# The first FFN and the input projection as bodies of one block, with waits at first use in place of the barrier between them

## What is computed

```python
x = x + 0.5 * ffn(layernorm(x))                 # weights = lut[idx], 256 -> 688 -> 256
x = x + mamba(layernorm(x))                     # the step in the middle
x = x + 0.5 * ffn(layernorm(x))                 # the same weights again

def ffn(x):    return (silu(x @ W_gate.T) * (x @ W_up.T)) @ W_down.T
def mamba(x):
    proj = x @ in_proj_w * mup                  # 256 -> z 512, xBC 768, dt 64
    xBC  = silu(causal_conv4(xBC) + conv_b)     # per channel, 4 taps
    dt   = softplus(dt + dt_bias)
    # scan over 2048 tokens, 64 heads of 8, state of 128; then + D * x,
    # rms norm, norm_w, * silu(z)
    return y @ out_proj_w                       # 512 -> 256
```

## Time and profile before

| what | value |
|---|---|
| median of 3 runs | 519.86 us (518.34 to 520.81) |
| the profiled execution | 518.19 us |
| its span, first to last instruction | 516.5 us |
| mean granted TensorE clock | 0.98 |
| PE busy | 473.5 us, 92% |
| DVE busy | 374.7 us, 73% |
| ACT busy | 284.0 us, 55% |
| GpSimd busy | 160.9 us, 31% |

### The profile page before, as it was taken

One profiled execution on the slowest core, in us unless ns is written; L12 is line 12 of the kernel. 1 busy time (PEld: TensorE's weight loads), 2 busy tenths in 40 slices (PEclk: granted clock), 3 DMA queues, 4 the chain that ended last, 5 costly groups with the idle time before them and its releaser, 6 DMA issues.

```text
span 516.5 us, 17146 instructions
## 1 busy us (share of the span) xinstructions
PE 473.5 (92%) x7486; PEld 396.9 (77%) x7486; DVE 374.7 (73%) x742; ACT 284.0 (55%) x513; POOL 160.9 (31%) x216
## 2 busy tenths in 40 slices
PE   4899999999989995986899999999978999999997
PEld 3557797988878884875688878887867778898987
DVE  7998936466769999844788888788859866556543
ACT  3658535253328999798556665567635423323241
POOL 1100040203042111114667676676746411000000
PEclk9999999999989999797999999999989999999999
DMA  8960080000000000100000000000350000101001
GB/s 206 207 241 1 1 339 7 0 3 1 0 1 0 3 0 0 42 22 3 4 6 4 5 4 6 4 5 4 134 220 4 4 2 0 42 7 35 22 21 42
DMA packets 7387, 21.31 MB, mean 41 GB/s; under 512 B 784, under 2 KB 5392, under 8 KB 6672
## 3 DMA queue, kind: packets, MB, share of 16 engines
q1 hardware_dynamic: 6832, 18.05, 10.7%
q10 hardware_dynamic: 480, 2.16, 1.8%
HBM read 12.87 MB, written 6.55 MB: 38 GB/s over the span
## 4 chain that ended last, share of the span: by engine, by line
PE 32%; issue 9%; POOL 8%; ACT 4%; DVE 3%; POOLq 0%; DVEq 0%; ACTq 0%
POOL w L1264 6%; PE intra L898 4%; PE seg L876 2%; PE yo L1016 2%; POOL tmp L1281 1%; PE XB L987 1%; PE new L999 1%; PE XB L68 1%; PE BG L68 1%; PE yo L70 1%; PE yo L68 1%; PE yo L69 1%; PE new L68 1%; PE XB L950 1%; PE new L70 1%
## 5 line engine op out<-in xcount | busy, mean ns | idle before, releaser
L1264 POOL TENSOR_TENSOR w<-xdt,ends 32x512 f32<-32x512 f32 (+3 forms) x63 | 66.5, 1074 | 4.2 <-PE prior L994 2.8
L657 DVE SCALAR_TENSOR_TENSOR cv<-pre,vec,cv 128x512 f32<-128x512 f32 x72 | 52.9, 750 | 5.5 <-ACT cv L695 3.8
L1043 ACT ACTIVATE seg<-seg 128x512 f32<-128x512 f32 x64 | 35.8, 578 | 32.6 <-PE seg L876 32.5
L1131 DVE TENSOR_TENSOR mmat<-seg,gs 128x512 f32<-128x512 f32 x64 | 42.5, 684 | 11.3 <-ACT seg L1043 11.3
L528 POOL TENSOR_TENSOR n_rstd<-n_ve,m_half 128x4 f32<-128x4 f32 x12 | 13.1, 1088 | 120.2 <-DVE n_ve L523 120.1
L876 PEld LDWEIGHTS seg<-abk,m_seg 96*32 96x32 bf16 x2048 | 20.7, 97 | 24.1 <-DVE mmat L1131 12.7
L68 PE MATMUL pj<-n_xT,win 128*128 128x512 f32 x88 | 35.6, 405 | 2.3 <-PEq L130 2.3
L1056 ACT ACTIVATE f_hT<-f_h 128x512 fp32r<-128x512 f32 (+1 forms) x24 | 15.2, 632 | 40.1 <-DVE f_h L1142 40.1
L69 PE MATMUL pj<-n_xT,win 128*128 128x512 f32 x88 | 35.0, 397 | 0.0
L876 PE MATMUL seg<-abk,m_seg 96*32 96x64 bf16 x2048 | 27.2, 196 | 8.4 <-ACT ends L1047 4.7
L70 PE MATMUL pj<-n_xT,win 128*128 128x512 f32 x88 | 34.8, 395 | 0.0
(11 more groups left out here) (264 smaller groups left out, 1454.9 us busy)
## 6 DMA issues: line engine op xcount, KB each, us to landing
wgu_dram<-wgu SPq DMA_DIRECT2D x1, 2816.0 KB, 8.2
wgu<-wgu_dram SPq DMA_DIRECT2D x1, 2816.0 KB, 10.5
out<-x_res SPq DMA_DIRECT2D x8, 256.0 KB, 2.1
x_res<-in_x SPq DMA_DIRECT2D x1, 1536.0 KB, 23.6
wd_dram<-wd SPq DMA_DIRECT2D x1, 1536.0 KB, 11.6
wd<-wd_dram SPq DMA_DIRECT2D x1, 1536.0 KB, 13.8
win_raw<-in_in_w SPq DMA_DIRECT2D x1, 1408.0 KB, 26.4
gu_idx<-in_gu ACTq DMA_DIRECT2D x3, 352.0 KB, 9.1
```

The costliest lines, as they stand in the source:

```text
L657: dve.scalar_tensor_tensor(dst, pre[:, x, k:k + GN].rearrange("p (t c) -> p t c", c=P), cw[:, x, k:k + 1], dst, ALU.mult, ALU.add).then_in ...
L1043: act.activation(seg[u_ % 2][:, :, :], seg[u_ % 2][:, :, :], ACT.Exp).then_inc(s["exp_ok"], 1)
L1131: dve.tensor_tensor(mmat[a % 2][:, i, :], seg[u_ % 2][:, :, :], gs[a % 2][:, i].unsqueeze(2).broadcast_to([P, IU, HEADS]), ALU.mult).then_ ...
L1264: pool.tensor_tensor(heads(w[r, n, :]), heads(xdt[a % 2][r, :]), ends[a % 2][r, n * HEADS:(n + 1) * HEADS].unsqueeze(2) .broadcast_to([Q * ...
```

## The change

`build_front` and `build_in_proj` no longer open blocks; they get one block from `build` and write their bodies into it. An engine's second body is joined to its first by a branch. The barrier between the stages (L130) is gone, the one behind the projection stays. In its place stand waits: DVE, ACT and GpSimd wait in the second bodies until all 8 down products are done, all 12 splits of GpSimd are made (a new semaphore `split_lo`) and both stores have landed; PE waits for the splits of `win`, and late in the stage, ahead of dt's transposes, for the last residual addition. Semaphores of the projection get names of their own. In GpSimd's first body the four splits of `wout` now come ahead of the root of group 2 (`GROUPS + 2`) and behind the same wait for the last `h_lo`.

```diff
--- before.py
+++ after.py
@@ -123,14 +123,13 @@
     return pe.matmul(out, hT[:, 0, c, tok], wd[:, 1, c, :], start=False, stop=True)
 
 
-def build_front(nc, T, A, norm):
+def build_front(nc, T, A, norm, block, sem):
 
 
 
     with ExitStack() as ctx:
         sb = lambda n, s, d=F32: ctx.enter_context(nc.sbuf_tensor(n, s, d))
         ps = lambda n, s: ctx.enter_context(nc.psum_tensor(n, s, F32))
-        sem = lambda n: ctx.enter_context(nc.semaphore(n))
         gu_idx, dn_idx = sb("gu_idx", [P, QTR, GUC * P], I32), sb("dn_idx", [P, HALVES + 1, HID], I32)
         lut_h, lut_l = sb("lut_h", [P, PAIRS], F32R), sb("lut_l", [P, PAIRS], F32R)
         two, table = sb("two", [P, H64]), sb("table", [P, PAIRS, 2, H64], F32R)
@@ -160,10 +159,12 @@
             "mask_ok", "amask_ok", "used_ok", "aused_ok", "evac_ok", "split_hi", "wout_s"))
         gate_ok, up_ok, silu_ok, h_ok, h_hi, h_lo, down_ok, res_ok, stored = map(sem, (
             "gate_ok", "up_ok", "silu_ok", "h_ok", "h_hi", "h_lo", "down_ok", "res_ok", "stored"))
+        split_lo = sem("split_lo")
+        T["ffn1_read"] = ((down_ok, GROUPS * GT // 2), (split_lo, 4 * KC + 4), (stored, 32))
+        T["ffn1_banks"], T["win_parts"] = (res_ok, GROUPS * GT // 2), ((split_hi, KC), (split_lo, 4 * KC))
         win, wout, wgu, wd, x_res = T["win"], T["wout"], T["wgu"], T["wd"], T["x_res"]
         x_in_dram = A["x"][0].rearrange("(t p) c -> p t c", p=P)
         UNITS = QTR + FCH
-        block = ctx.enter_context(nc.Block())
 
         def rows(c):
             return P if c < FCH - 1 else FLAST
@@ -233,14 +234,16 @@
                 for part in range(4):
                     c = slice(part * PCH * P // 4, (part + 1) * PCH * P // 4)
                     pool.tensor_tensor(win[:, 1, k, :, :].rearrange("p c n -> p (c n)")[:, c], win_raw[:, k, c],
-                                       win[:, 0, k, :, :].rearrange("p c n -> p (c n)")[:, c].bitcast(F32), ALU.subtract)
+                                       win[:, 0, k, :, :].rearrange("p c n -> p (c n)")[:, c].bitcast(F32), ALU.subtract
+                                       ).then_inc(split_lo, 1)
             norm.pool_rstd(pool, GROUPS)
             norm.pool_rstd(pool, GROUPS + 1)
-            norm.pool_rstd(pool, GROUPS + 2)
             pool.wait_ge(h_lo, GROUPS * FCH)
             pool.wait_ge(split_hi, KC + 1)
             for k in range(4):
-                pool.tensor_tensor(wout[:, 1, k, :], wout_raw[:, k, :], wout[:, 0, k, :].bitcast(F32), ALU.subtract)
+                pool.tensor_tensor(wout[:, 1, k, :], wout_raw[:, k, :], wout[:, 0, k, :].bitcast(F32), ALU.subtract
+                                   ).then_inc(split_lo, 1)
+            norm.pool_rstd(pool, GROUPS + 2)
 
         @block.vector
         def _(dve):
@@ -559,11 +562,13 @@
         pe.wait_ge(self.lo_ok, (g + self.base) * KC + kc + 1 + KC)
 
 
-def build_in_proj(nc, T, norm):
+def build_in_proj(nc, T, norm, block, sem):
+
 
     with ExitStack() as ctx:
         sb = lambda n, s, d=F32: ctx.enter_context(nc.sbuf_tensor(n, s, d))
-        sem = lambda n: ctx.enter_context(nc.semaphore(n))
+        stage_sem = sem
+        sem = lambda n: stage_sem("pj_" + n)
         norm.base = GROUPS
         HALO = KCONV - 1
         H = GN // 2
@@ -608,13 +613,18 @@
                   (LAST, CONV_C[5]), (B4, 3), *((LAST, c) for c in range(4))]
         AT = {chunk: n for n, chunk in enumerate(ORDER)}
         TRANSPOSE_BEHIND = CONV_C[1]
-        block = ctx.enter_context(nc.Block())
 
         def conv_out(g, x):
             return cv[:, g * GT:g * GT + GT, x, :]
 
+        def ffn1_places(engine):
+
+            for read, count in T["ffn1_read"]:
+                engine.wait_ge(read, count)
+
         @block.vector
         def _(dve):
+            ffn1_places(dve)
             dve.tensor_scalar(cw[:, :, :], cw[:, :, :], MUP_X, None, ALU.mult).then_inc(w_ok, 1)
             dve.memset(pre[:, :, 0:HALO], 0.0).then_inc(carry_ok, XCH)
             dve.wait_ge(w_ok, 1)
@@ -663,6 +673,7 @@
         @block.gpsimd
         def _(pool):
             norm.pool_rstd(pool, LAST)
+            ffn1_places(pool)
             for g in range(LAST):
                 if g == 0:
                     pool.memset(T["xbd"][:, :, :, :], 0.0).then_inc(T["blank"], 1)
@@ -675,6 +686,7 @@
         @block.scalar
         def _(act):
             act.wait_ge(w_ok, 1)
+            ffn1_places(act)
 
             def silu(g, n):
 
@@ -753,6 +765,8 @@
         @block.tensor
         def _(pe):
             x_hi, x_lo = norm.xT[:, 0], norm.xT[:, 1]
+            for parts, count in T["win_parts"]:
+                pe.wait_ge(parts, count)
             for n, (g, c) in enumerate(ORDER):
                 if n >= 4:
                     pe.wait_ge(ev_ok, n - 3)
@@ -766,6 +780,7 @@
                     norm.pe_transpose(pe, g + 1)
                 if (g, c) == (LAST, CONV_C[2]):
                     pe.wait_ge(norm.lo_ok, 2 * GROUPS * KC + KC)
+                    pe.wait_ge(*T["ffn1_banks"])
                     pe.wait_ge(A_ok, 1)
                     pe.wait_ge(dt_ok, 1)
                     for t in range(GROUPS * HT):
@@ -1346,15 +1361,17 @@
         with ExitStack() as win_s:
             norm = Norm(nc, win_s, T, "n1_", side="right", banks=[T["new"], T["prior"]])
             put(win_s, ("win", [P, 2, KC, PCH, P], F32R), side="right")
-            with ExitStack() as ffn1:
-                put(ffn1, *ffn_w)
-                build_front(nc, T, A, norm)
+            sem = lambda n: win_s.enter_context(nc.semaphore(n))
             mamba = ExitStack()
-            put(mamba, *mamba_t)
-            T["abk_in"], T["blank"] = (mamba.enter_context(nc.semaphore(n)) for n in ("abk_in", "blank"))
-            for name in ("intra", "yo"):
-                T[name] = mamba.enter_context(nc.psum_tensor(name, [P, INTER], F32, side="right"))
-            build_in_proj(nc, T, norm)
+            T["abk_in"], T["blank"] = (base.enter_context(nc.semaphore(n)) for n in ("abk_in", "blank"))
+            with nc.Block() as block:
+                with ExitStack() as ffn1:
+                    put(ffn1, *ffn_w)
+                    build_front(nc, T, A, norm, block, sem)
+                put(mamba, *mamba_t)
+                for name in ("intra", "yo"):
+                    T[name] = mamba.enter_context(nc.psum_tensor(name, [P, INTER], F32, side="right"))
+                build_in_proj(nc, T, norm, block, sem)
         build_scan(nc, T, norm2, out)
         mamba.close()
```

## The result

The changed kernel took 513.8 us in the median of 11 executions (512.46 to 518.32), the kernel before 519.84 in the median of 11 (516.74 to 520.81). The ratio is 0.9921, with a 95% interval of 0.9892 to 0.9949, that is 4.1 us faster, between 2.7 and 5.6. In a later series the same two kernels gave 0.9953 (0.9923 to 0.9984), 2.4 us. The ratio is not that of the two medians (0.9884), which lie 6.0 us apart; the means, 514.95 and 519.27, lie 4.3 us apart. Of the changed kernel's executions seven took 512.5 to 515.1 us and four 516.5 to 518.3, so I go by the ratio and not by the median. The forecast of 3.4 us lies between the two ratios.

A forecast was written before the change was run, and what follows sets the result against it. The prediction took DVE to bound the projection, its first tap held by the barrier; the tap's 3.3 us became 3.4 at dt's end and reached the end, 519.86 - 3.4 = 516.4 us, own range 514.4 to 517.6, asked range 514.0 to 519.1.

The forecast's parts named there:

- What holds the barrier: Between first FFN and projection: GpSimd's four output-weight splits, 2.78 us, end last at 150.56; moving them is worth 1.2 us.
- PE: At the hand-over: first projection matmul at 148.33 instead of 150.81, clock stays high; PE gains 4.2 us.
- DVE sets the tap, not ACT: First tap of the projection: DVE's own queue puts it at 151.7 instead of 155.03, a gain of 3.3 us.
- The new waits at nothing: Second bodies: waits at first use and twelve new increments cost nothing; DVE's wait ends 0.4 us before ACT's chunk.
- The move at nothing: GpSimd's output-weight splits at 143.2 to 146.0 neither delay the root of group 2 nor slow DVE; cost taken as nothing.
- PE's lead dies: Projection up to dt: PE's 4.2 us lead shrinks to DVE's 3.3; 3.4 us taken at 206.6.
- Behind dt: Low clock after the wait for dt: 0.9 us lost or 0.8 won, with later dips 1.6 us either way.
- The sum: Whole kernel: 3.4 us gained, from a median of 519.86 to 516.4 us, or 0.65%.
- A fetch behind the branch, short or long: Rivals at the second bodies: instruction fetch stalls. Short: 518.4 us, chance 0.10. Long, over about 2.5 us: 521.4, chance 0.05.
- GpSimd did not slow DVE: Rival at the moved splits: the 2.8 us in which GpSimd and DVE overlap doubles; gain 0.5, 519.4 us, chance 0.04.
- The waits did not hold both engines: Rival at the new waits: some count is met only at about 150.5, holding DVE and PE; 519.9 us, chance 0.04.
- The clock took nothing back: Rival on the clock: low stretches fall worse on work by 1.6 us; 518.0 us, chance 0.12.

The follow-up runs named there:

- the move alone: Kernel before, with GpSimd's four output-weight splits put ahead of the root of group 2, block and barrier kept; ratio 0.9941.
- the block alone: Changed kernel with GpSimd's output-weight splits back in their old place behind the root of group 2; ratio 0.9933, run again for a trace 0.9946.
- the barrier rebuilt out of waits: Changed kernel with the splits back behind the root, and PE too waiting for all places before its first projection matmul; ratio 0.9978.
- changed, again: The changed kernel unchanged, run a second time in a later series against the kernel before; 517.6 us, ratio 0.9953.
- before, PE filled: Kernel before, with nine matmuls of unused result behind the last down product, barrier and splits unchanged; ratio 0.9970.
- two chunks moved: Changed kernel with dt's transposes on PE two chunks later; ratio to the kernel before 0.9882, in a second run 515.94 us and 0.9906.
- dt later: Changed kernel with dt's transposes on PE two chunks later (ratios to the kernel before 0.9882 and 0.9906) or three chunks later (0.9894).

## Why the prediction was right

The mechanism at the hand-over came out as it was put, step by step; two sizes were off there, and what was won behind dt may be luck.

*What holds the barrier.* GpSimd's splits: taking them forward alone gives 2.47 of 3.65 us. Shown by the move alone.

*PE.* First matmul 0.11 us behind the last down product (0.12 forecast), clock at 1.00, ACT's first copy 1.75 us behind the first matmul (1.57 forecast: 149.9 less 148.33), because ACT followed the sixth matmul by 0.58 us (148.24 to 148.82) and not by 0.44.

*DVE sets the tap, not ACT.* Forecast 151.7 less 149.22, 2.48 us behind the additions; measured 2.16. The term was over by 0.3: the branch and three waits cost nothing that can be seen (the scaling starts before the additions' modelled end, 147.88 against 147.97), where I had allowed 0.13, and the tap followed the last statistic by the queue's ordinary overlap, where I had added its full length. The two are nearly level, since ACT ends the first chunk at 149.31 + 0.78 = 150.09 and DVE starts at 150.13. That DVE's own queue sets the tap is shown by the block alone: there ACT's second instruction starts at 153.40, 1.44 us ahead of the tap (0.82 here), and from scaling to tap DVE takes 2.26 us, as here 2.25. That a shorter queue of DVE alone would have gained next to nothing is argued from the near level, not shown.

*The new waits at nothing.* Shown for DVE and PE by their rows, and by the barrier rebuilt out of waits: what costs is the slowest engine, whatever mechanism waits for it.

*The move at nothing.* The statistics beside the splits took 1.39 us at 143.15 in the changed kernel, against 1.40 in the kernel before, and the root of group 2 started 2.62 us ahead of the additions' end, against 2.61 before.

*PE's lead dies.* Tap to dt is 51.3 us in eight of ten traces, whether PE has its whole lead of 4 us (block alone) or starts with DVE (move alone); DVE's taps set that stage. The two traces in which the clock fell at the hand-over have 51.57 and 51.83. The 0.24 us that went is more than my 0.1, and it isn't the wait that I had named. That one, 0.22 us at a tap at 171.25, is gone, but one of 0.15 us at a later tap (182.25) stands in its stead; up to there the two kernels run level, 32.13 and 32.12 us behind the first tap. The difference stands where DVE starts on dt, 44.79 and 44.55 us behind it: before, DVE waited there for ACT's exponential, whose end at 199.78 is 44.75 us behind the tap. DVE's timeline with all engines held by waits has this wait in brackets:

```profile
200.10 0.69 DVE L640 TENSOR_SCALAR dl<-w 128x1024 f32<-128x1024 f32 x1 [0.17 <-ACT w L729]
```

*Behind dt.* I had allowed 0.9 us lost or 0.8 won by where the low clock lies on work and taken zero. It was 0.81 won in the first pair of traces. Of the low stretch before, 5.7 us lay on work and not the "some 5" of the prediction, so more could be won than I had said. In seven traces the low stretch around dt's end lasted about 6.8 us each time; how much of it lay behind dt's end, from the granted clock of the stretches there, orders them:

```text
                        low after dt's end   dt to scan
changed, again                3.2              20.90
before, PE filled             3.7              21.19
changed                       4.0              21.34
move alone                    4.0              21.27
block alone (again)           5.5              22.03
before                        5.7              22.15
waits hold all                6.2              22.37
```

Half a microsecond for each microsecond at half rate. Whether the change makes the stretch end sooner or the executions fell so is open: block alone has full clock at the hand-over and 5.5, so a clock that stays up there does not by itself bring it forward, and the move alone and the filled kernel, both with the barrier, have 4.0 and 3.7, so the missing barrier isn't needed for it.

*The sum.* 3.4 us forecast; 4.55 in the first pair of traces, of which 0.8 may be chance; 4.1 and 2.4 by the two ratios. To dt's end, where the prediction had put its 3.4 us, the change gave 3.65 + 0.24 = 3.89. The prediction's own range, 514.4 to 517.6, does not follow from the 1.6 us either way that it allowed: around 516.4 that is 514.8 to 518.0.

*The rivals.* A fetch behind the branch, short or long, did not occur: no engine of either trace of the changed kernel pauses there. The rule of the Trainium skill that I weighed (Runtime: NRT & Kernel Launch, Instruction fetch mechanics) makes the stall depend on a target outside the fetched window; that none was seen in 0.11 us between matmuls on PE agrees with a second body that follows the first, which no trace shows directly. GpSimd did not slow DVE: from the first statistics to the end of the additions, with the splits in between, DVE took 130.01 us, against 130.06 before. The waits did not hold both engines, though block alone shows how near that rival was: with the splits left in place, DVE was held 1.31 us by the very list of places. The clock took nothing back in either trace of the changed kernel; that is two executions, and whether it must be so is as open as the cause above.

## What to carry to other kernels

Before a barrier is taken away, read who drains last: if it is one engine with work that could stand elsewhere, moving that work can give most of the gain (here 2.5 of 3.65 us), and without the move the waits that take the barrier's place wait for the same work. Follow the lead of each engine to the next place where it meets the bounding one; a lead of over 4 us on PE was worth what DVE's queue let through. And where an engine has a long wait with independent work behind it, splitting the wait can pay twice when the clock would fall in it: two chunks moved won 2.65 us, 1.73 of them because the products behind the wait ran at full rate, although another engine bounded the tail.

## What the runs showed of the hardware

Pauses of PE at the hand-over of 2.31 and 2.34 us were followed by 3.4 us at half rate; pauses of 1.06 and 0.30 us were not. The three traces with dt later had a pause of 1.85 to 1.87 us a chunk or two ahead of dt's products, and the clock stayed at full rate around dt's end; the seven others waited 6.1 us for dt and had 6.8 us at half rate, begun in the wait.

The ten traces, one execution each, differ most in two places that the change does not touch. The first loads: DVE's first statistics lie between 18.0 and 21.1 us, with the same code before them. And the scan: from its start to the end it took 287.75 to 292.26 us with the same code. Low clock explains little of it. The kernel before was the fastest there with 6.8 and 3.4 us of low clock in the scan, the move alone had 3.4 and 3.4 and was 2 us slower.
